# Call lists of a period laid out anew, with small products standing between full-tile ones

## The reference, cut to what matters

```python
q = _short_conv(hidden_states @ Wq.T, conv_q).reshape(b, t, H, DK)
k = _short_conv(hidden_states @ Wk.T, conv_k).reshape(b, t, H, R, DK)
v = _short_conv(hidden_states @ Wv.T, conv_v).reshape(b, t, H, R, DV)
...
M = jnp.tril(M, k=-1)
kexp = kg * jnp.exp(Gg)[:, :, :, None, :]
rhs = (vg - jnp.einsum('bhtid,bhdv->bhtiv', kexp, S)).reshape(b, h, C * Rr, dv)
u = jax.scipy.linalg.solve_triangular(M, rhs, lower=True, unit_diagonal=True)
...
S_new = jnp.exp(glast)[..., None] * S + jnp.einsum('bhtid,bhtiv->bhdv', kdec, u)
```

## Time and profile before

| | us |
|---|---|
| median of 3 runs (4885.9 to 4906.08) | 4895.43 |
| span of the profiled execution, first to last instruction | 4882.9 |
| median less span: what lies around it, and the difference between runs | 12.5 |
| busy PE, DVE, ACT, POOL | 4493.2, 4052.7, 3391.0, 3362.7 |
| one steady period (from one `take` of DVE to the next), full clock | 67.0 |
| one with a slow stretch of PE | 68.5 |

### The profile page before, as it was taken

How to read it: one execution, slowest core, us unless ns; L and a number is a source line. 1 busy time by engine, 2 the same in 40 slices (tenths; PEclk the granted TensorE clock), 3 DMA queues, 4 the chain that set the end, 5 groups by cost and what they waited for, 6 DMA issues and landing times.

```text
span 4882.9 us, 151877 instructions
## 1 busy us (share of the span) xinstructions
PE 4493.2 (92%) x63200; PEld 3127.3 (64%) x63200; DVE 4052.7 (83%) x7262; ACT 3391.0 (69%) x6708; POOL 3362.7 (69%) x5828
## 2 busy tenths in 40 slices
PE   8869999999999999999999999999999999999888
PEld 4536666666666666666666666666666666666655
DVE  3279999989998989889988899889999899988622
ACT  3267777777777777777777777777777777777531
POOL 0047777777777777777777777777777777777600
PEclk9989999999999999999999999999999999999899
DMA  2200000000100000000100000000000000000100
GB/s 88 88 29 25 26 26 26 15 25 26 34 32 16 28 26 26 26 14 26 35 32 28 15 26 26 26 25 14 30 30 26 26 14 26 26 26 9 37 9 22
DMA packets 49727, 135.48 MB, mean 28 GB/s; under 512 B 7056, under 2 KB 28176, under 8 KB 48400
## 3 DMA queue, kind: packets, MB, share of 16 engines
q1 hardware_dynamic: 49040, 125.77, 7.3%
HBM read 111.60 MB, written 14.16 MB: 26 GB/s over the span
## 4 chain that ended last, share of the span: by engine, by line
PE 58%; DVE 26%; ACT 9%; issue 6%; POOL 1%; DMA 0%; DVEq 0%; SPq 0%; ACTq 0%
PE bank L835 49%; DVE acc L1556 9%; PE bank L302 7%; DVE X L1553 6%; PE bank L906 2%; DVE Rs L1556 2%; DVE Pd L1661 2%; ACT o L1182 1%; DVE sp_t L1553 1%; DVE Zc L1740 1%; ACT Us L1181 1%; DVE o L1556 1%; ACT acc L1181 1%; ACT L1471 1%; ACT Ztf L1181 1%
## 5 line engine op out<-in xcount | busy, mean ns | idle before, releaser
L1556 DVE SCALAR_TENSOR_TENSOR acc<-bank,vc,acc 128x510 f32<-128x510 f32 (+2 forms) x1728 | 1270.9, 739 | 145.5 <-ACT acc L1181 120.0
L2006 POOL TENSOR_TENSOR LZ<-LZ,LT 128x120 f32<-128x120 f32 (+26 forms) x1984 | 979.5, 494 | 155.5
L2003 POOL TENSOR_TENSOR LT<-LA,LZ 128x120 f32<-128x120 f32 (+26 forms) x1984 | 877.8, 442 | 145.8
L1553 DVE TENSOR_TENSOR X<-KQ,Fl 128x640 f32<-128x640 f32 x1024 | 966.6, 960 | 0.9 <-ACT Fl L1182 0.9
L1976 POOL COPY X<-KQ 128x640 f32<-128x640 f32 x256 | 255.9, 1000 | 807.5 <-ACT F L1182 278.3
L835 PEld LDWEIGHTS bank<-X 128*32 128x32 f32 x32768 | 524.0, 112 | 301.0 <-issue 210.8
L1181 ACT ACTIVATE Us<-bank 128x128 f32<-128x128 f32 x1024 | 280.7, 277 | 627.8 <-PE bank L835 617.3
L835 PE MATMUL bank<-X 128*32 128x60 f32 (+1 forms) x32768 | 650.3, 205 | 64.4 <-issue 32.6
L835 PE MATMUL bank<-xnTm,WK 128*128 128x512 f32 x1280 | 660.8, 642 | 41.5 <-DVE acc L1556 35.8
L1951 POOL TENSOR_TENSOR kdec<-KQ,Fe 128x256 f32<-128x256 f32 x512 | 461.0, 921 | 152.3 <-PE bank L906 152.3
L835 PE MATMUL bank<-Rs,Ztf 128*128 128x128 f32 x2048 | 460.7, 312 | 68.1 <-DVE Rs L1556 48.0
(11 more groups left out here) (144 smaller groups left out, 9204.1 us busy)
## 6 DMA issues: line engine op xcount, KB each, us to landing
WK<-in_wkq SPq DMA_DIRECT2D x64, 704.0 KB, 6.1
WV<-in_wv SPq DMA_DIRECT2D x64, 576.0 KB, 3.9
WO<-in_wo SPq DMA_DIRECT2D x64, 128.0 KB, 2.0
wuh<-in_wu SPq DMA_DIRECT2D x2, 1024.0 KB, 7.5
xt<-in_x SPq DMA_DIRECT2D x4, 512.0 KB, 6.2
wuh_d<-wuh SPq DMA_DIRECT2D x1, 2048.0 KB, 6.3
x_d<-x SPq DMA_DIRECT2D x4, 512.0 KB, 3.0
xnT_d<-xT SPq DMA_DIRECT2D x4, 512.0 KB, 2.7
```

Source lines behind the costliest of these rows:

```text
L1553: return e.tensor_tensor(o, a, b, op)
L1556: return e.scalar_tensor_tensor(out=o, in0=a, scalar=sc, in1=b, op0=op0, op1=op1)
L2003: e.tensor_tensor(tmp, LA[:, j + 1:32, 8 * (j % R) + j // R].unsqueeze(2).broadcast_to([P, rr, cc]), LZ[:, j, 0:cc].unsqueeze(1).broadcast ...
L2006: e.tensor_tensor(LZ[:, j + 1:32, 0:cc], LZ[:, j + 1:32, 0:cc], tmp, SUB).then_inc(g_row, 1)
```

## The change

The four lists are written in another order, and `bank_use` and `acc_use` follow it. No call is added or taken away. Several calls cross the end of the loop body (`rhs(0,3)` of PE, `tap_k(1)`, `keep(3)` and `solve(0,2)` of ACT, `distance(3)` and others of DVE), with their step shifted to match. The diff, cut to what the prediction speaks of:

```diff
@@ bank_use @@
-            ("vturn", 2, 2, a_vt, 4, 2), ("turn", 0, 1, a_kdT, 4, 0), ("norm", 0, 0, v_max, 1, 0),
-            ("vturn", 3, 2, a_vt, 4, 3), ("turn", 1, 1, a_kdT, 4, 1), ("k", 0, -1, v_ck, 15, 2),
+            ("vturn", 2, 2, a_vt, 4, 2), ("turn", 0, 1, a_kdT, 4, 0), ("vturn", 3, 2, a_vt, 4, 3),
+            ("norm", 0, 0, v_max, 1, 0), ("turn", 1, 1, a_kdT, 4, 1), ("k", 0, -1, v_ck, 15, 2),
@@ delta_tensor, start of the body @@
-                rhs(p - 3, 0, 3)
-                products(p - 1, 0, 1)
+                spare(p - 3, 7)
+                update(p - 3, 1, 2)
                 solve(p - 3, 0, 3)
...
                 project_k(p, 2)
-                rhs(p - 3, 0, 4)
                 solve(p - 3, 1, 3)
+                products(p - 1, 0, 2)
                 spare(p - 3, 10)
-                solve(p - 3, 0, 4)
                 update(p - 3, 1, 3)
                 spare(p - 3, 11)
-                update(p - 3, 0, 4)
+                solve(p - 3, 0, 4)
                 rhs(p - 3, 1, 4)
                 project_v(p - 1, 0)
-                products(p - 1, 0, 2)
+                update(p - 3, 0, 4)
...
-                products(p - 1, 0, 4)
                 solve(p - 3, 0, 6)
                 rhs(p - 3, 1, 6)
+                products(p - 1, 0, 4)
                 solve(p - 3, 1, 6)
...
                 rhs(p - 3, 0, 7)
+                rhs(p - 3, 1, 7)
                 project_v(p - 1, 1)
                 solve(p - 3, 0, 7)
-                rhs(p - 3, 1, 7)
+                solve(p - 3, 1, 7)
                 project_k(p, 3)
-                solve(p - 3, 1, 7)
@@ delta_tensor, inversion @@
                 products(p - 1, 2, 1)
+                products(p - 1, 2, 2)
+                products(p - 1, 2, 3)
                 project_v(p - 1, 3)
+                spare(p - 2, 30)
                 first(p - 2, 0)
-                spare(p - 2, 30)
-                products(p - 1, 2, 2)
+                products(p - 1, 2, 4)
+                spare(p - 2, 31)
                 second(p - 2, 0)
-                spare(p - 2, 31)
-                products(p - 1, 2, 3)
                 turn_v(p - 2, 1)
-                products(p - 1, 2, 4)
                 third(p - 2, 0)
-                spare(p - 2, 32)
                 turn_v(p - 2, 2)
                 turn(p - 1, 0)
+                spare(p - 2, 32)
+                products(p - 1, 3, 0)
+                products(p - 1, 3, 1)
+                turn_v(p - 2, 3)
+                spare(p - 2, 33)
+                products(p - 1, 3, 2)
                 fourth(p - 2, 0)
...
                 third(p - 2, 1)
+                rhs(p - 2, 0, 1)
                 spare(p - 2, 36)
-                update(p - 2, 0, 0)
+                fourth(p - 2, 1)
                 project_k(p + 1, 1)
-                fourth(p - 2, 1)
                 spare(p - 2, 37)
-                rhs(p - 2, 0, 1)
                 solve(p - 2, 1, 0)
+                solve(p - 2, 0, 1)
@@ delta_scalar @@
+                tap_k(p, 1)
+                spare(p - 3, 1)
+                update(p - 3, 1, 0)
+                keep(p - 2, 3)
...
                 silu_k(p, 0)
-                silu_k(p, 1)
...
-                e.preload_act_table_set("natural_log_exp_and_others")
-                length(p - 2, 1)
-                factors(p - 1, 4)
...
+                factors(p - 1, 4)
                 solve(p - 3, 0, 4)
+                tap_v(p - 1, 0)
...
                 solve(p - 3, 1, 5)
-                spare(p - 3, 16)
+                e.preload_act_table_set("natural_log_exp_and_others")
...
+                second(p - 2, 0)
+                silu_v(p - 1, 2)
+                turned_v(p - 2, 1)
+                silu_v(p - 1, 3)
+                keep(p - 1, 2)
+                spare(p - 2, 32)
+                third(p - 2, 0)
+                turned_v(p - 2, 2)
                 square(p)
...
                 fourth(p - 2, 1)
+                factors(p, 1)
                 spare(p - 2, 37)
+                factors(p, 2)
                 solve(p - 2, 1, 0)
@@ delta_vector @@
+                conv_v(p - 1, 0, 0)
                 update(p - 3, 0, 6)
...
                 conv_k(p, 4, 1)
+                evacuate(p - 1, 1, 0)
                 conv_k(p, 4, 0)
-                evacuate(p - 1, 1, 0)
+                evacuate(p - 1, 1, 1)
+                softplus(p)
                 output(p - 3, 0)
...
+                lengths(p - 2)
                 evacuate(p - 1, 2, 2)
+                evacuate(p - 1, 2, 3)
                 levels(p - 1, 3, 1)
-                softplus(p)
+                spare(p - 2, 32)
                 levels(p - 1, 3, 2)
-                evacuate(p - 1, 2, 3)
-                clamp(p)
-                lengths(p - 2)
@@ delta_gpsimd @@
-                spread(p - 1, 0, 0)
                 spread(p - 1, 0, 1)
                 spread(p - 1, 1, 1)
+                spread(p - 1, 0, 0)
                 spread(p - 1, 1, 0)
+                spread(p - 1, 2, 0)
                 spread(p - 1, 2, 1)
-                spread(p - 1, 2, 0)
```

More of the change, by code:

```diff
@@ L1121, in delta_tensor @@
                 third(p - 2, 0)
-                spare(p - 2, 32)
                 turn_v(p - 2, 2)
                 turn(p - 1, 0)
+                spare(p - 2, 32)
[4 more added lines that the diff above has]
+                products(p - 1, 3, 2)
                 fourth(p - 2, 0)
-                spare(p - 2, 33)
                 total(p)
-                turn_v(p - 2, 3)
-                products(p - 1, 3, 0)
+                turn(p - 1, 1)
@@ L1130, in delta_tensor @@
+                spare(p - 2, 34)
+                products(p - 1, 3, 3)
                 first(p - 2, 1)
-                spare(p - 2, 34)
-                products(p - 1, 3, 1)
-                turn(p - 1, 1)
+                products(p - 1, 3, 4)
+                spare(p - 2, 35)
+                solve(p - 2, 0, 0)
                 second(p - 2, 1)
-                spare(p - 2, 35)
-                products(p - 1, 3, 2)
-                products(p - 1, 3, 3)
-                solve(p - 2, 0, 0)
@@ L1151, in delta_tensor @@
                 update(p - 2, 1, 0)
+                update(p - 2, 0, 1)
                 spare(p - 2, 2)
-                update(p - 2, 0, 1)
                 rhs(p - 2, 1, 1)
+                rhs(p - 2, 0, 2)
+                products(p, 0, 0)
+                solve(p - 2, 1, 1)
                 turn(p - 1, 2)
-                rhs(p - 2, 0, 2)
-                solve(p - 2, 1, 1)
+                solve(p - 2, 0, 2)
                 spare(p - 2, 4)
@@ L1160, in delta_tensor @@
                 spare(p - 2, 5)
-                solve(p - 2, 0, 2)
+                products(p, 0, 1)
                 rhs(p - 2, 1, 2)
                 update(p - 2, 0, 2)
-                products(p, 0, 0)
                 solve(p - 2, 1, 2)
-                spare(p - 2, 7)
+                rhs(p - 2, 0, 3)
         def delta_scalar(e, ffn):
@@ L1805, in delta_vector @@
             for p in range(-1, NS + 3):
+                distance(p - 1, 3)
+                rhs(p - 3, 1, 1)
+                rhs(p - 3, 0, 2)
+                levels(p - 1, 0, 1)
+                conv_k(p, 1, 2)
+                spare(p - 3, 4)
+                spare(p - 3, 5)
+                update(p - 3, 1, 1)
                 conv_k(p, 1, 1)
+                rhs(p - 3, 1, 2)
+                update(p - 3, 0, 2)
                 spare(p - 3, 7)
@@ L1809, in delta_vector @@
                 conv_k(p, 1, 0)
-                levels(p - 1, 0, 2)
                 update(p - 3, 1, 2)
@@ L1814, in delta_vector @@
                 update(p - 3, 0, 3)
+                rhs(p - 3, 1, 3)
+                rhs(p - 3, 0, 4)
+                levels(p - 1, 0, 2)
                 levels(p - 1, 0, 3)
-                rhs(p - 3, 1, 3)
-                diagonal(p - 2)
-                rhs(p - 3, 0, 4)
-                conv_k(p, 2, 2)
+                distance(p - 1, 5)
                 spare(p - 3, 10)
                 update(p - 3, 1, 3)
-                distance(p - 1, 5)
                 spare(p - 3, 11)
+                conv_k(p, 2, 2)
                 rhs(p - 3, 1, 4)
                 conv_k(p, 2, 1)
+                diagonal(p - 2)
                 update(p - 3, 0, 4)
@@ L1928, in delta_vector @@
                 update(p - 2, 0, 1)
-                rhs(p - 2, 1, 1)
-                distance(p, 3)
-                rhs(p - 2, 0, 2)
-                levels(p, 0, 1)
-                spare(p - 2, 4)
-                update(p - 2, 1, 1)
-                conv_k(p + 1, 1, 2)
-                spare(p - 2, 5)
-                rhs(p - 2, 1, 2)
-                update(p - 2, 0, 2)
         def delta_gpsimd(e):
```

173 lines of the change are left out of this document (79 added, 94 removed).

## The result

The changed kernel takes 4863.6 us (median of 4 runs, 4858.0 to 4879.3) where the kernel before, run beside it, takes 4897.6: ratio 0.9937, interval 0.9916 to 0.9959. That is 0.6% faster, at the edge of what a measurement can tell. I had forecast 4972, slower by 77 us.

A forecast was written before the change was run, and what follows sets the result against it. It took no single engine to bound a period (chain 58% PE, 26% DVE), with about 4 us of PE slack. Terms summed to +1.2 us per period, x 64 = +77, giving 4972 us; range 4805 to 5040.

The forecast's parts named there:

- Term 5: Chunk stage: PE waits of 1.02 in all go, new ones of 0.2, 0.2 and 0.35 come; -0.2 us per period.
- Term 1: Softplus and one evacuation ahead of DVE's output(0), on which PE's gate stands: +0.6 us per period.
- Term 2: products(2,4) before second, (2,2) and (2,3) before project_v(3): PE waits about 0.65 before third; +0.5 us per period.
- Term 3: Third quarter's end: keep(2) and turned_v(2) come late, a PE wait of 0.35 goes; +0.2 us per period.
- Term 4: Around fourth(1): the 0.26 wait goes, new waits of 0.35 and 0.2 come; +0.3 us per period.
- Term 6: End of the recurrence: the stop before mean_square stays, the wait behind it for conv_k(3) shrinks; -0.2 us per period.
- Term 7: Edits with no cost: one more ACT table load per step, 1.3 us, is covered by PE's project_k(2) and what follows.
- DVE rival: DVE sets the inversion stage's pace, hiding terms 1 to 4: about -1.3 us per period, 4812 us; chance 0.30.
- deciding mark: In the inversion: products(3,0) starting earlier than now against project_v(2) decides whether DVE sets the pace.
- trade of waits: Whole kernel: new waits equal the old ones, so the time stays the same, 4895 us; chance 0.17.
- clock rival: New stops push each period into a 1.2 GHz stretch: +52 us on the forecast, 5024 us; chance 0.07.
- proof of error: Period below 67 us, PE's idle time under 4 us with the same busy time, or no stop before third.

## Why the prediction was wrong

**Term 5, the chunk stage, is the step that failed.** I took -0.2 and measured -1.50: 1.01 of idle time and 0.49 of busy time. The waits that go were right, 1.02 by my rows. Two other parts were not. First, the new waits of 0.2, 0.2 and 0.35, 0.75 in all: there is one of 0.11 before update(1,2), that before update(1,4) is 0.11 and was 0.14 before, and rhs(0,7) has none. With 0.06 that also goes before solve(0,3), the idle time comes to -1.03 - 0.06 - 0.03 + 0.11 = -1.01. I had put the new waits in by the order of PE's list alone ("solve and update of one half stand next to each other"), without working out when ACT and DVE, whose lists had changed too, would be done. The run with PE's list alone shows how large such waits are where the other lists do not follow. Second, I put the change of PE's busy time at nothing. The words "this is all that a new order of the same calls can win" took PE's busy time as fixed, and the bound of -1.0 held idle time only. It fell by 0.49 in this stage. Some 0.2 of that are starts at 0.49 for 0.38, of which there are two fewer (the earlier trace rows had the 0.49 in them, and I had no row beside them for the same matmuls in full flow); the rest has no cause shown. The run with four products calls put back shows that it is the small products in the gaps that do both: it brings back 1.24 of idle and 0.45 of busy time. With -1.5 in term 5 the sum is -0.1 per period: no change that a measurement could tell, and not yet the gain.

**Term 1** was right in kind, +0.43 for +0.6, with gate and project_v(2) waiting as described, and 0.66 when softplus goes back. Its size owes something to luck: a stop of 0.29 before products(1,0), in this piece, went at the same time. What softplus costs in the whole kernel is less, 0.34 per period, through the levels.

**Term 2** was right about its wait (0.70 for 0.65) and too small: +1.17 for +0.5. I missed first's wait for place(3) and that for levels(2,3).

**Term 3** had the wrong sign, -0.47 for +0.2. The piece after third took 9.89 to 12.23 before (median 10.32) and 9.85 in nearly every period after. DVE was busy 10.17 of the 10.32, so it may have paced it; no run shows that alone. Softplus isn't what mattered: put back into this stretch, with DVE busy 9.34 there, it leaves the piece at 9.85. turned_v(2) is late as I said and costs the 0.29 in front of turn_v(3). The 0.20 in front of products(3,0) has no releaser in the trace; ACT's keep(2) ends 0.10 before it. Together they cost less than what goes: idle time falls from 0.83 to 0.49.

**Term 4** was right in its waits and wrong in its sum: idle time rises by 0.29 for +0.3 (a stop of 0.26 before fourth(1), 0.44 for 0.14 before update(1,0), and the 0.26 before solve(1,0) gone), but the busy time falls by 0.28, and the piece changes by +0.02. It is the error of term 5 over again.

**Term 6** was +0.10 for -0.2: the wait before project_k(4), which was to shrink, grew from 0.43 to 0.56. **Term 7** held: the added load is free, as far as it was tested.

**The rivals.** The DVE rival had the sign. Its mark, softplus near 0.7, came (0.69), and its time of 4812 was too low. Its deciding mark came too, but decides nothing: products(3,0) starts 2283.42 - 2271.69 = 11.73 behind project_v(2), against 2213.42 - 2200.11 = 13.31, because fourth, total and turn_v(3), 2.98 with the stop, no longer stand ahead of it. project_v(2) to project_k(p+1,0) as a whole is 0.70 longer, so terms 1 to 4 were not hidden, and the new inversion alone makes the kernel slower. The gain is in the chunk stage, to which the rival gave only -0.4 with term 6. The trade of waits, 4895, missed by 31 us. The clock rival did not come: 20 of 49 periods touched a stretch at 1.2 GHz after, 17 before, and one costs 1.04 now and 1.14 then. What I named as proof of error, the period below 67 us, stood at the edge (66.99), but the 67.0 that I compared with was a short one: at full clock the median period is 67.5 before and 67.0 after. PE's idle time, which I wanted at 4 us or more, is 4.9 per period, so stops did come, in less busy time.

The range of 4805 to 5040 holds the result, by its lower end, which I had drawn for the DVE rival and not for this.

## What to carry to other kernels

Where four queues are written by hand, a wait forecast from one list alone is a guess: work out when the other lists deliver, in time, or keep its lower end at nothing. A stop of PE costs here its idle time and about 0.1 us more in the matmuls behind it, so filling a gap with small work that has to be done anyway is worth more than the gap shows. PE's busy time is no constant of the work: it depends on the order, and a sum over waits alone misses that. And before a call is moved up, ask who waits for what it overtakes, and which operation of another engine it will now run beside.

## What the runs showed of the hardware

**DVE and POOL slow each other down, and being early can cost time.** A levels operation (128x640, two inputs from SBUF) takes 0.82 with POOL at rest and 1.2 to 1.35 beside one of its tensor operations; softplus 0.68 and 1.22. The middle one of three rows of the changed kernel shows the other side, with softplus at 2268.44 for 0.69:

```profile
2268.25 0.30 POOL L2006 TENSOR_TENSOR LZ<-LZ,LT 128x56 f32<-128x56 f32 x1
2268.63 0.63 POOL L2003 TENSOR_TENSOR LT<-LA,LZ 128x45 f32<-128x45 f32 x1
2269.34 0.28 POOL L2006 TENSOR_TENSOR LZ<-LZ,LT 128x45 f32<-128x45 f32 x1
```

POOL's operation of 0.63 takes 0.27 or 0.28 in most periods, and it ends 0.13 after softplus does. It looks held up until DVE is through. That isn't the rule, though: in the same period levels(2,4) and POOL's product for level(3) overlap, and both take 1.33, where they take 0.82 and 0.75 otherwise. The Trainium skill (SBUF — State Buffer, Who interferes with whom) has a DVE instruction with two SBUF inputs contend with a GpSimd one that reads SBUF; the trace agrees that the two contend, with the numbers above. What that makes of a schedule is the part I had not expected: two edits that brought project_v(2) forward by 0.66 and 0.46 us moved the two engines onto each other and lost 0.56 in the levels, and the second made the kernel 46 us slower. A third, softplus moved where it meets no POOL operation, got the same meeting from DVE being late, and cost 47 us.

**More stops did not mean a slower clock.** The two kernels with the old stops in the chunk stage and the new inversion (four products calls back, and the new inversion alone) show 3 and 2 periods of 49 with a stretch at 1.2 GHz, against 20 in the changed kernel's trace. That trace is its slowest execution: the mean granted clocks of all executions are 0.983 to 0.985 and 0.982 to 0.984 for those two, and 0.974, 0.979, 0.981 and 0.983 for the changed kernel. So much of the difference is between executions, and what is left is small. I can't say why, and tried nothing for it. In the traces it is worth some 0.3 us per period, 20 x 1.04 / 49 = 0.42 in the changed kernel against 0.09 with the products calls back.
